# A graph kernel's 512-wide layer: four of its 50 blocks summed by count tiles beside the gathers, one gather buffer, and a table of halves for the last layer

## The reference

```python
def _gin_conv(h, src, dst, w, b, eps, n_nodes):
    agg = jax.ops.segment_sum(h[src], dst, num_segments=n_nodes)
    return ((1.0 + eps) * h + agg) @ w + b

h = jax.nn.relu(_gin_conv(x, src, dst, w1, b1, eps1, n))   # 256 -> 512
h = jax.nn.relu(_gin_conv(h, src, dst, w2, b2, eps2, n))   # 512 -> 512
return _gin_conv(h, src, dst, w3, b3, eps3, n)             # 512 -> 256
```

## Time and profile before

| | us |
|---|---|
| three runs: median (lowest to highest) | 4474.14 (4473.64 to 4477.79) |
| the profiled execution: its own time | 4474.49 |
| the profiled execution: span of the trace | 4472.9 |
| wide layer, first gather issued to last store issued | 2758.5 to 3843.3 |
| last layer, first gather issued to end of span | 3852.6 to 4472.9 |

### The profile page before, as it was taken

The page is one execution under the profiler, slowest core; times in us unless marked ns, Lnnn a source line. Parts: engine busy times, 40 slices in busy tenths (PEclk is TensorE's granted clock), DMA queues, the critical chain, the costliest instruction groups (busy, mean ns, idle before and its releaser), DMA issues. The chain is left out here.

```text
span 4472.9 us, 70047 instructions
## 1 busy us (share of the span) xinstructions
PE 3582.4 (80%) x16651; PEld 2364.0 (53%) x16652; DVE 2070.7 (46%) x7633; ACT 1206.9 (27%) x2400; POOL 2622.6 (59%) x2830
## 2 busy tenths in 40 slices
PE   3876557777777779876999997888888888589998
PEld 1223345555555557764777774334333443367776
DVE  6987667777777773462222221222222222323332
ACT  3972122222222221362333331000000000222222
POOL 5001177777777760035666664777777777477775
PEclk9999977788777779957999998999999999799999
DMA  4432144444444430167888885777777777666665
GB/s 140 173 155 58 49 111 111 113 113 112 111 112 112 111 95 0 37 183 217 245 242 244 245 244 158 227 227 226 225 231 228 227 227 227 179 199 205 209 203 172
DMA packets 352295, 749.76 MB, mean 168 GB/s; under 512 B 82289, under 2 KB 161183, under 8 KB 348872
## 3 DMA queue, kind: packets, MB, share of 16 engines
q0 software_dynamic: 208336, 538.34, 42.4%
q10 hardware_dynamic: 72332, 112.04, 7.9%
q1 hardware_dynamic: 71529, 98.27, 6.7%
HBM read 654.57 MB, written 93.84 MB: 167 GB/s over the span
## 5 line engine op out<-in xcount | busy, mean ns | idle before, releaser
L1721 POOL DMA_INDIRECT l_gathered<-table,record x850 | 815.2, 959 | 400.7 <-issue 275.5
L2081 POOL DMA_INDIRECT l_gathered<-table,record x850 | 812.2, 956 | 303.6 <-issue 298.4
L814 POOL DMA_INDIRECT a_gathered<-table,record x850 | 810.2, 953 | 303.6 <-issue 254.7
L2175 PE MATMUL bank<-l_gathered,l_onehot 128*125 128x512 f32 x1700 | 804.3, 624 | 167.2 <-DMA l_gathered<-table,record 166.9
L2175 PEld LDWEIGHTS bank<-l_gathered,l_onehot 128*125 128x125 f32 x1700 | 323.0, 196 | 621.7 <-issue 351.6
L1138 PE MATMUL bank<-a_gathered,a_onehot 128*125 128x264 f32 x1700 | 523.3, 468 | 75.7 <-DVE a_gathered L942 75.7
L1138 PEld LDWEIGHTS bank<-a_gathered,a_onehot 128*125 128x125 f32 x1700 | 376.4, 230 | 172.6 <-DVE a_gathered L942 50.8
L1851 ACT ACTIVATE l_part<-l_packed 128x1000 fp32r<-128x1000 bf16 (+1 forms) x300 | 313.8, 1071 | 527.5 <-PE bank L1932 423.6
L1951 PE MATMUL bank<-l_gathered,l_onehot 128*125 128x256 f32 (+1 forms) x1275 | 329.3, 415 | 80.6 <-DMA l_gathered<-table,record 80.6
L2114 DVE SCALAR_TENSOR_TENSOR l_z<-l_own,one_eps,bank 125x512 f32<-125x512 f32 x50 | 37.4, 747 | 707.3 <-PE bank L2182 707.3
L1932 PE MATMUL bank<-rows_first,l_part 125*125 125x512 f32 x1250 | 307.6, 405 | 29.0 <-ACT l_part L1851 29.0
(11 more groups left out here) (265 smaller groups left out, 4968.2 us busy)
## 6 DMA issues: line engine op xcount, KB each, us to landing
l_packed<-adjacency ACTq DMA_DIRECT2D x200, 250.0 KB, 5.1
adjacency<-d_stage SPq DMA_DIRECT2D x25, 1562.5 KB
l_packed<-adjacency ACTq DMA_DIRECT2D x100, 281.2 KB, 6.0
l_gathered<-table,record POOLq DMA_INDIRECT x1700, 3.7
a_gathered<-table,record POOLq DMA_INDIRECT x850
table<-rows_first POOLq DMA_DIRECT2D x50, 250.0 KB, 3.6
table<-l_work ACTq DMA_DIRECT2D x50, 250.0 KB
l_own<-table SPq DMA_DIRECT2D x50, 250.0 KB
```

What stands on the lines that cost most here:

```text
L814: pool.indirect_dma_start(out=gathered0[s][:, j * TW:(j + 1) * TW], out_offset=None, in_=table0, in_offset=bass.IndirectOffsetOnAxis(ap=re ...
L1721: pool.indirect_dma_start(out=gathered[g][:, j, :], out_offset=None, in_=table, in_offset=bass.IndirectOffsetOnAxis(ap=record[k.t][:, j, 0 ...
L2081: pool.indirect_dma_start(out=gathered[s][:, j * w:(j + 1) * w], out_offset=None, in_=table, in_offset=bass.IndirectOffsetOnAxis(ap=record ...
L2175: last = pe.matmul(sum_ps[s][0:NB, 0:w], onehot[s][:, j, :], rows[:, j, :], start=False, stop=(j == T - 1), skip_group_check=True)
```

## The change

1. In the wide layer the last four odd blocks (43, 45, 47, 49; `TABLED`) are summed by count tiles, in the four PSUM banks 4 to 7. This is spread over the steps: `source_sums` takes one source block per step, eight steps ahead (`AHEAD`), and multiplies its two halves by the four blocks' count tiles (eight matmuls of 512 columns). For it ACT loads the source rows (250 KB, `load_source`) and every fourth time the count tiles (`load_parts`), casts a tile and the upper half (`cast_source`), and DVE cuts the rows (`split_source`). Six source blocks are done before PE's first gathered sums, two more behind them.
2. The wide layer has one gather buffer instead of two, and one PSUM bank each for `turn` and `down`.
3. The results of the wide layer are cut into halves there (`halve` on DVE, `keep_upper` on ACT), kept in SBUF as `rows_last`, and `table3` gets both halves (2 KB per row, twice as much as before).
4. The last layer takes `rows_last` as it is: the loads, the cutting and the own rows' loads go. Its gathers fetch halves: 2 KB instead of 1 KB per row, in one buffer, and one fp32r pass instead of an fp32 product. As in the first layer, the order within a pair of blocks becomes odd (count tiles), then even (gathered).
5. The weights of the wide layer are loaded by ACT behind the first source blocks, no longer by SP.

The core of the diff:

```diff
+TABLED = 4
+AHEAD = 8
...
-    table3 = nc.dram_tensor("table3", (N, D), F32).ap()
+    table3 = nc.dram_tensor("table3", (N, 2 * D), F32).ap()
...
-            halves = not last_layer
-            row_width = 2 * D if halves else D
-            kind = F32R if halves else F32
+            halves = True
+            row_width, kind = 2 * D, F32R
...
-                rows_sb = rows_first if halves else phase.enter_context(nc.sbuf_tensor(f"l{n}_rows", [NB, BLOCKS, 2 * D], F32R))
+                rows_sb = rows_last if last_layer else rows_first
...
-                gathered = [t[:, :] for t in tiles("gathered", [P, T * w])]
-                sum_ps, turn_ps, product_ps = banks[0:2], banks[2:4], banks[4:6]
+                gathered = phase.enter_context(nc.sbuf_tensor(f"l{n}_gathered", [P, T * w], F32))[:, :]
+                sum_ps, turn_ps, product_ps, tabled_ps = banks[0:2], banks[2], banks[3], banks[4:8]
...
+                    def split_source(r, a, u):
+                        v = u * 2 + a // 2
+                        dve.wait_ge(rows_loaded[r], v * 16 + 16)
...
+                        dve.wait_ge(source_used[r], v + 1)
+                        order.step(dve.tensor_scalar(source_cut[:, :].bitcast(I32), source_rows[r][:, :].bitcast(I32), HIGH, None, ALU.bitwise_and))
+                        dve.sem_inc(rows_cut, 1)
+                        order.step(dve.tensor_tensor(source[r][:, w:2 * w], source_rows[r][:, :], source_cut[:, :], ALU.subtract))
+                        dve.sem_inc(rows_split[r], 1)
...
+                    over_steps(dve, [(rounds_of, 0), (finish, 1), (halve, 4)], split_source, 6)
...
+                    def keep_upper(s, i):
+                        act.wait_ge(upper_cut[s], i + 1)
+                        act.activation(rows_last[:, bass.ds(2 * i + s, 1), 0:D].rearrange("p o c -> p (o c)"), upper[s][:, :],
+                                       ACT.Copy).then_inc(upper_ready[s], 1)
+                        act.wait_ge(upper_ready[s], i + 2)
+                        act.wait_ge(lower_ready[s], i + 2)
+                        act.dma_start(block_rows(table3, 2 * i + s),
+                                      rows_last[:, bass.ds(2 * i + s, 1), :].rearrange("p o c -> p (o c)").bitcast(F32)).then_inc(stored[s], 16)
...
+                    def cast_source(r, a, u):
+                        v = u * 2 + a // 2
+                        act.wait_ge(part_loaded, u * 16 + 16)
+                        act.wait_ge(source_used[r], v + 1)
+                        act.activation(part[r][:, :, :], packed[:, :, a * NB:(a + 1) * NB], ACT.Copy).then_inc(part_cast[r], 1)
+                        act.wait_ge(rows_cut, v * 2 + r + 1)
+                        act.activation(source[r][:, 0:w], source_cut[:, :], ACT.Copy).then_inc(upper_cast[r], 1)
...
+                            load_source(r, u * 4 + a + 2)
...
+                    over_steps(act, [(load_weights, 0), (copy_turned, 1), (store, 2), (keep_upper, 5)], cast_source, AHEAD)
...
+                    def source_sums(r, a, u):
+                        v = u * 2 + a // 2
+                        first = isinstance(u, int) and u == 0 and a == 0
+                        pe.wait_ge(part_cast[r], v + 1)
+                        pe.wait_ge(rows_split[r], v + 1)
+                        pe.wait_ge(upper_cast[r], v + 1)
+                        for d in range(TABLED):
+                            for half in range(2):
+                                last = pe.matmul(tabled_ps[d][0:NB, 0:w], part[r][0:NB, d, :], source[r][:, half * w:(half + 1) * w],
+                                                 start=(first and half == 0), stop=False, skip_group_check=True)
+                        last.then_inc(source_used[r], 1)
...
-                    over_steps(pe, [(rounds_of, 0), (turn, 1), (down, 2)])
+                    over_steps(pe, [(rounds_of, 0), (turn, 1), (down, 2)], source_sums, 6)
```

More of the change, by code:

```diff
@@ L1677, in load_own @@
                             sp.dma_start(x1_sb[k.s][:, :], block_rows(x1, k.b)).then_inc(x1_loaded[k.s], 16)
[L1679 to L1691, removed]
+                    over_steps(sp, [(load_records, 0), (load_x1, 1)], load_weights)
                 @block.gpsimd
@@ L2010, in wide_layer @@
                 zT = tiles("zT", [P, k_tiles, NB])
-                result = tiles("result", [NB, D])
+                result, upper = tiles("result", [NB, D]), tiles("upper", [NB, D])
                 weights_loaded = sem(f"l{n}_weights_loaded")
@@ L2022, in step, with total_of, over_steps @@
+                def total_of(s, i):
+                    return tabled_ps[i - (PAIRS - TABLED)] if tabled(s, i) else sum_ps[s]
+                def over_steps(engine, stages, beside=None, early=0):
                     def step(b, j=0):
                         for stage, lag in stages:
-                            if 0 <= b - lag < BLOCKS:
-                                stage((b - lag) % 2, j + (b - lag) // 2)
-                    for b in range(4):
+                            if b >= first_step and 0 <= b - lag < BLOCKS:
+                                stage((b - lag) % 2, 2 * j + (b - lag) // 2)
+                        if beside is not None and b < BLOCKS - AHEAD:
+                            beside(b % 2, b % 4, j + (b + AHEAD) // 4)
+                    first_step = 0
+                    if beside is not None:
+                        for m in range(early):
+                            beside(m % 2, m % 4, m // 4)
+                        for stage, lag in stages:
+                            if lag == 0:
+                                stage(0, 0)
+                        for m in range(early, AHEAD):
+                            beside(m % 2, m % 4, m // 4)
+                        first_step = 1
+                    for b in range(6):
@@ L2087, in _ @@
+                    over_steps(pool, [(gather, 0)])
                 @block.vector
@@ new lines, in cast_source @@
+                    def cast_source(r, a, u):
[5 more added lines that the diff above has]
+                        act.activation(source[r][:, 0:w], source_cut[:, :], ACT.Copy).then_inc(upper_cast[r], 1)
+                        static = isinstance(u, int)
+                        if not static or 4 * u + a + 2 < BLOCKS:
+                            act.wait_ge(rows_split[r], v + 1)
+                            load_source(r, u * 4 + a + 2)
+                        if a == 3 and (not static or 4 * u + 4 < BLOCKS):
+                            for k in range(2):
+                                act.wait_ge(part_cast[k], u * 2 + 2)
+                            load_parts(u + 1)
```

331 lines of the change are left out of this document (199 added, 132 removed).

## The result

The kernel takes 4455.58 us (median of 6 runs, 4450.91 to 4465.58) against 4474.32 us before (6 runs): ratio 0.9962, 95% interval 0.995 to 0.9973. It is faster by 18.7 us, 0.4%, where 34 were forecast. The profiled execution took 4454.23 us, with a span of 4452.6.

A forecast was written before the change was run, and what follows sets the result against it. PE was taken to become the wide layer's bound, with the last layer near POOL's pace. Wide layer -9 and last layer -25 us, from 4474.5, gave 4440 us; 8 in 10 for 4375 to 4520.

The forecast's parts named there:

- PE's step, 23.1 us: Wide layer: PE's time per full step with source products, waits and low clock, above POOL's 21.4; range 21.9 to 24.0.
- PE's wait: Wide layer, each step: PE idle for ACT's chain of copies, store issue and casts before source_sums; 2.7 us, from 1.1 to 3.5.
- low clock: Wide layer: PE's loss to reduced clock, kept at 1.2 us per block because the new wait replaces those for rows.
- The 0.3 us for value loads: Wide layer, each step: gap because PE's value loads for the next block start only behind its wait; bounded by 0 and 0.5.
- this upper end: Wide layer: every wait pays low clock in full, step 24.0 us, total 4478, no change; chance 0.10.
- PE's first gathered block near 2775: Start of the wide layer: PE does six source blocks first, so its first gathered block starts about 7 us later than before.
- The tail, 89 us: Last eight wide-layer steps, from PE's start on block 42: 25.5 us, two pairs of 22.6, landing 2.8, last quarter 4.6, drain 10.5.
- From the last store to the last layer, 9.3 us as before: Between wide layer's last store and POOL's first instruction of the last layer: 9.3 us, unchanged from the kernel before.
- The last layer, 595.6: From POOL's first instruction to the end: 25 pairs of 23.3 us plus the ending, 595.6 against 620.3, saving 25.
- the 68 saved gathers are nearly all given back: Wide layer: 86 us of POOL saved, 71 us lost to 42 steps 1.7 longer; the layer ends 9 us earlier.
- POOL as the bound: Rival, wide layer: ACT's chain is shorter or overlapped, step stays 21.4 us, layer ends about 3766, total 4372; chance 0.15.
- few DMA engines saturate: Rival: 125-row transfers on five engines give wide-layer steps of 24.2 us and last-layer pairs up to 25.9; total 4552, chance 0.22.

The follow-up runs named there:

- e5: e1 with each wide-layer transfer of 125 rows (own rows, source rows, stores) made as two, of 112 and 13 rows; 4381.2 us.
- e7: The edits of e5 and e6 together on the changed kernel; 4367.6 us, ratio 0.9763 to the kernel before.
- e2: The changed kernel with all 50 wide-layer blocks gathered, without source blocks or count tiles there; 4438.6 us.
- e1: The changed kernel with ACT's two casts for source_sums ahead of the copies and the store in each wide-layer step; 4400.9 us.
- e9: e7 with four source blocks instead of six ahead of PE's first gathered block; 4366.0 us.
- e6: e1 with SP loading own rows a step later and DVE making one-hot tiles of blocks 44, 46, 48 right behind the preceding small block's; 4397.8 us.

## Why the prediction was half right

The forecast ended the span at 4439.1 by its own terms (2775 + 970.2 + 89 + 9.3 + 595.6); it ended at 4452.6.

- **PE's step, 23.1 us: right** (22.96). So was its make-up: PE's wait 2.6 for 2.7 on average, the casts and copies each within 0.1 us. PE is busy 852.86/42 = 20.3 us per step where 17.0 and 1.9 were counted at full clock, so low clock cost 1.4 us, a little more than the 1.2 taken, and it sat where the wait is, on the source products (2.79 us for 1.9) more than on the gathered ones (699.1/46 = 15.2 for 14.6). The 0.3 us for value loads did not show (1.3 us in all before `L2290`). Together -6 us against the forecast. Low clock did not come with each wait; two steps in a row of the kernel after, timeline, and a window behind the second wait:

```profile
3725.29 2.10 PE L2317 MATMUL bank<-l_source,l_part 125*125 125x512 f32 x8 [2.42 <-ACT l_source L2239]
...
3747.28 3.65 PE L2317 MATMUL bank<-l_source,l_part 125*125 125x512 f32 x8 [2.42 <-ACT l_source L2239]
```

```profile
3748.00:3749.00 1.00, 1.00 (x3) 0.73 (x3) 0.29 (x2) 0.00 (x0) 0.69 (x2) 0.50 0.84 249
```

  So the step did not stand at 24.0, and the mean granted clock stayed at 0.95. The prediction took this upper end to be what the Trainium skill says (TensorE: Matmul & The Clock Gate, "HAM oscillation"). That section is about a loop that waits 3 to 5 us after every 2 us or so of matmuls; a wait of 2.6 us in a step of 23 is not that loop, so the steps here don't test what it says.
- **PE's first gathered block near 2775: the first step that failed**, by 11 us (2786.4), although the first gather came 10 us earlier. The prediction gave the six source blocks 1.9 to 3.8 us each of PE's time; they took 28 us, at the pace of their loads. Start of the kernel after:

```profile
2756.65 0.62 ACT L2237 ACTIVATE l_part<-l_packed 128x500 fp32r<-128x500 bf16 x1 [19.91 <-DMA l_packed<-adjacency]
...
2779.44 0.62 ACT L2237 ACTIVATE l_part<-l_packed 128x500 fp32r<-128x500 bf16 x1 [7.69 <-DMA l_packed<-adjacency]
...
2792.07 0.94 POOL L2107 DMA_INDIRECT l_gathered<-table,record  x1 [21.85 <-PE bank L2297]
```

  In the loop a source block is loaded two steps ahead; at the start nothing lies between its load and its use. e5 shows which part is the five engines: 8.5 us. The kernel before opened its second block 28.5 us after the first gather, the kernel after 59.2, and e7 still 47.4, so even the best start here costs some 19 us more than one without source blocks.
- **The tail, 89 us: failed by 19** (108.1). It was worked out along POOL: two pairs of 22.6 behind gather 44. POOL was first held by a record that stood in SP's queue behind an own-row load (7.99 us), then by PE (5.85), and PE three times by one-hot tiles (11.4 us in all). Each of these is an order in one engine's program that a full step hides and a small block doesn't. e7's 101.1 is the nearest that the runs came to 89.
- **From the last store to the last layer, 9.3 us as before: failed by 6** (15.4). The store was doubled by the change, and the prediction charged it in the steps and not at the barrier, where nothing covers it. e5 gives it back.
- **The last layer, 595.6: right in kind, 17 us too dear** (578.4). From POOL's first instruction at 3874.22 to its last at 4441.09 it is 22.7 us per pair, the lower end of the forecast's bounds, not 23.3, and 10.6 us follow the last gather, not 13.1. The saving is 42 us instead of 25. PE waits for rows (82.3 us between 3904 and 4440, 43.8 before) and the clock is 0.88, but none of that reaches POOL.

The sum of these: +11.4 - 5.9 + 19.1 + 6.1 - 17.2 = +13.5 us. That the total missed by so little is luck: terms that were 37 us too cheap met others that were 23 us too dear. The right sign rested on the last layer. The sentence that the 68 saved gathers are nearly all given back was too kind: by e2 they were given back with 17 us on top.

Of the rivals, POOL as the bound was wrong for this kernel and right for e1 (its sum, 2775 + 42 x 21.4 + 89, is 3762.8 and not 3766). That few DMA engines saturate was right in its mechanism and wrong in its place: five engines carry each 125-row transfer, which costs 15 us at start and gap (e5 against e1), and nothing in a step of 21.5 us, where such a transfer has all the step to land. What stays open is the rest of the start: with the loads split 26.6 us still pass there, and a second buffer for the count tiles' loads, which e9 points to, was not tried.

## What to carry to other kernels

Work that is put beside a pipeline must be asked of each engine before the things that engine does late, not after: one swapped pair of calls was worth 55 us, three times the gain of the whole change. Price the two ends of a stage by themselves, along every engine, with transfers in the open; a term that is hidden in the loop is paid there in full. And when an edit shows nothing, try it again once its neighbour's wait is gone (e6 alone 3 us, within the spread of the runs; on top of the split 14).

## What the runs showed of the hardware

- With nothing else under way, stores of 125 rows keep about 0.33 of the DMA engines busy; cut into 112 and 13 rows they reach 0.8 to 0.9. The time from the last store to the next stage's first gather fell from 15.2 to 9.0 us (e1, e5).
- A record load of 34 KB issued behind a 250 KB one in the same queue was usable after 10.8 us (e6), behind a split one after 5.5 (e7).
- POOL's gathers kept one per 1.26 us at a DMA share of 1.02 and 292 GB/s.
- After waits of the same length, 2.42 us, the same eight matmuls took 2.10 us at full clock in one step and 3.65 in the next, where the granted clock fell to 0.50.
